# A decoder of six sublayers on one core: counting the next sequence's choices inside the FFN, and a new order of the pieces of two streams

## The reference

```python
x = _layernorm(x + mamba(x))                        # x: 16 sequences x 256 tokens x 256
x = _layernorm(x + latent_xattn(x, ctx, indices))   # indices: 16 x 256 x 64 choices of keys
x = _layernorm(x + ffn(x))                          # layernorm, int8-like quantisation, gelu
x = _layernorm(x + self_attention(x))
x = _layernorm(x + cross_attention(x, ctx))
x = _layernorm(x + moe(x))                          # 6 of 8 experts, and a shared one
```

## Time and profile before

| what | value |
|---|---|
| median of 3 runs | 4313.35 us (4283.68 to 4314.45) |
| the profiled execution, time | 4321.18 us |
| the profiled execution, span from first to last instruction | 4319.4 us |
| mean granted clock | 0.827 |
| TensorE / VectorE / ScalarE / GpSimd busy | 82% / 69% / 45% / 15% |

### The profile page before, as it was taken

The page is one execution under the profiler, slowest core; times in us unless marked ns, Lnnn a source line. Parts: engine busy times, 40 slices in busy tenths (PEclk is TensorE's granted clock), DMA queues, the critical chain, the costliest instruction groups (busy, mean ns, idle before and its releaser), DMA issues.

```text
span 4319.4 us, 57512 instructions
## 1 busy us (share of the span) xinstructions
PE 3553.2 (82%) x21234; PEld 2309.6 (53%) x21250; DVE 3000.4 (69%) x6506; ACT 1938.5 (45%) x4415; POOL 650.9 (15%) x516
## 2 busy tenths in 40 slices
PE   2668888888888888888888888878888888888977
PEld 1345645555565655645555564655645555564644
DVE  6586786848678585785858768586785858678532
ACT  2245454544545444453544535444453544545423
POOL 1112030301203021030200203011030201203000
PEclk7568989787897877888788888989888797897878
DMA  7233261514416152261523516153261524417101
GB/s 237 77 93 120 73 187 59 169 59 124 130 54 186 69 142 84 80 186 52 155 73 103 152 54 184 42 155 100 87 180 52 160 68 123 132 58 204 42 14 39
DMA packets 205689, 470.84 MB, mean 109 GB/s; under 512 B 23712, under 2 KB 43808, under 8 KB 190688
## 3 DMA queue, kind: packets, MB, share of 16 engines
q1 hardware_dynamic: 205408, 467.17, 35.7%
HBM read 446.11 MB, written 20.97 MB: 108 GB/s over the span
## 4 chain that ended last, share of the span: by engine, by line
PE 59%; DVE 26%; ACT 7%; issue 5%; DMA 3%; POOL 0%; SPq 0%; DVEq 0%; POOLq 0%; ACTq 0%
PE ps L593 7%; PE ps L574 5%; DVE region_x L1351 5%; PE ps L761 4%; PE ps L815 4%; PE ps L605 4%; PE ps L775 4%; PE ps L742 3%; PE ps L681 3%; PE ps L796 3%; DVE region_x L1338 3%; PE ps L464 3%; DMA region_x<-rows_of_dt 3%; PE ps L521 2%; DVE nm L1388 2%
## 5 line engine op out<-in xcount | busy, mean ns | idle before, releaser
L1148 POOL TENSOR_TENSOR region_x<-region_x 128x512 f32<-128x512 f32 x512 | 650.7, 1271 | 3327.8 <-DVE region_x L1351 3327.8
L1351 DVE TENSOR_TENSOR_SCAN region_x<-ps,region_x 128x512 f32<-128x512 f32 x512 | 622.6, 1216 | 67.0 <-ACT ps L965 67.0
L965 ACT ACTIVATE ps<-region_x,aneg 128x255 f32<-128x255 f32 x1024 | 443.2, 470 | 492.8 <-DVE region_x L1351 369.9
L1338 DVE TENSOR_TENSOR region_x<-region_x,ps 128x512 f32<-128x512 f32 x512 | 342.0, 668 | 42.8 <-PE ps L521 22.9
L1384 DVE CUSTOM_DVE_ANT_0 region_x<-ps,mask 128x256 f32<-128x256 f32 x512 | 185.9, 420 | 219.8 <-issue 219.4
L1075 ACT ACTIVATE region_y<-ps,rmax 128x256 f32<-128x256 f32 x512 | 235.2, 480 | 218.9 <-DVE rmax L1476 218.9
L815 PE MATMUL ps<-xTy,wide 128*128 128x256 f32 x1280 | 316.9, 397 | 3.5 <-DVE region_y L1535 3.5
L593 PE MATMUL ps<-region_y 32*128 32x256 f32 x1024 | 235.3, 601 | 86.5 <-ACT region_y L1001 52.3
L1401 DVE SCALAR_TENSOR_TENSOR region_x<-region_x,cntk 128x512 f32<-128x512 f32 x256 | 165.3, 687 | 196.5 <-ACT region_x L1001 196.5
L815 PEld LDWEIGHTS ps<-xTy,wide 128*128 128x128 f32 x1280 | 242.0, 196 | 52.9 <-issue 15.0
L1091 ACT ACTIVATE region_y<-ps 128x512 f32<-128x512 f32 x256 | 140.7, 595 | 284.7 <-PE ps L764 284.7
(11 more groups left out here) (244 smaller groups left out, 6632.2 us busy)
## 6 DMA issues: line engine op xcount, KB each, us to landing
region_x<-rows_of_dt SPq DMA_DIRECT2D x1024, 256.0 KB, 4.7
wide<-in_wgate SPq DMA_DIRECT2D x16, 1280.0 KB, 5.7
wide<-in_wup SPq DMA_DIRECT2D x16, 1280.0 KB, 8.4
down<-in_wmoe SPq DMA_DIRECT2D x16, 1280.0 KB, 5.5
wide<-in_wq SPq DMA_DIRECT2D x16, 1024.0 KB, 4.7
wide<-in_wk SPq DMA_DIRECT2D x16, 1024.0 KB, 7.4
wide<-in_wv SPq DMA_DIRECT2D x16, 1024.0 KB, 9.5
down<-in_wo SPq DMA_DIRECT2D x16, 1024.0 KB, 4.8
```

Source lines behind the costliest of these rows:

```text
L965: last = f(ps[:, 1 + 2 * (k % 2), m * T + 1:(m + 1) * T], dt_rep[k % SLOTS][:, m, 1:T], ACT.Exp, scale=aneg[:, k, m:m + 1])
L1148: nc.gpsimd.tensor_tensor(hbuf[k % HSLOTS], hbuf[k % HSLOTS], csb.unsqueeze(1).to_broadcast([P, 2, T]), ALU.mult).then_inc(hc_ready, 1)
L1338: tt_(hbuf[k % HSLOTS], dtx_rep[k % SLOTS], ps[:, 2, 0:T].unsqueeze(1).to_broadcast([P, 2, T]), ALU.mult).then_inc(dbx, 1)
L1351: nc.vector.tensor_tensor_scan(flat(hbuf[k % HSLOTS]), ps[:, 1 + 2 * (k % 2), :], flat(hbuf[k % HSLOTS]), 0.0, ALU.mult, ALU.add).then_inc ...
```

## The change

**Counting.** `digits` and `one_hots` of sequence i+1 now stand in `ffn` of sequence i on VectorE (digits and quarter 0 ahead of `f_h`, quarter 1 behind it, quarters 2 and 3 behind the quantisation), the 128 small matmuls in TensorE's `ffn` (quarters 0 and 1 behind w1, with a wait for both `f_h`; quarter 2 behind w2) and, quarter 3, behind the first projection of `mamba`. Their copies on ScalarE move alike. Turning the table, the mask and the last copy stay in `mamba`. Sequence 0 is counted before anything else.

**In-projection.** Its first two pieces no longer wait for `X.sum_read`; only the third does. The FFN's last sum and norm (`ffn_end`) run in two pieces inside the next `mamba` on VectorE, around the convolution.

**dt.** Low-rank part and rows of C are separate pieces, dt comes before B's columns, softplus's `sp_u` is made before Ln is there. SyncE stores the first half, reads back four units, and stores the second half then; the read waits for the first half only (units 0 to 15 use only that). In the scans the product of the next unit and the scan are separate pieces.

**Order.** Before, self-attention of y began with the low-rank part of the next-but-one `mamba`, and MoE ran beside the end of latent attention and the beginning of the FFN. Now y begins when that `mamba` has turned its counts. On TensorE: all of q, k, v and six score pieces come ahead of the first sum over states; cross-attention's output (L796) and the router come behind latent attention's output; the gate and up products stand beside the FFN's w1, counting and w2; the down product comes ahead of the last turning of the counts. On VectorE: self-attention's eight maxima stand between scans 1 and 6, its output pieces behind scans 19, 21 and 22, cross-attention's residual in the first norm of the FFN, MoE's products between the pieces of the FFN, MoE's residual in the middle of softplus, and `s.QT` (L1450) ahead of the first product. On SyncE the load of `wo2` stands between units 0 and 1 of the read-back, the store of the output at unit 8.

```diff
@@ first_half on SyncE @@
+                yield from store_half(0)
                 for k in range(UNITS):
...
+                    if k == SLOTS:
+                        yield from store_half(1)
+                    if k == 0 or k == UNITS // 2:
+                        sp.wait_ge(dt_stored[0], at(i, 32, 16 if k == 0 else 32))
@@ mamba on TensorE @@
+                pe.wait_ge(xT_loaded, at(i, 16, 16))
+                projected(0)
+                if i:
+                    yield from counted(i, 3, 4)
+                else:
+                    yield
+                yield
+                projected(1)
                 yield
                 if i:
                     pe.wait_ge(X.sum_read, at(i - 1, 3, 3))
+                projected(2)
...
+                pe.wait_ge(cnt_sb, at(i, 4, 4))
+                projected(3)
...
+                yield from counts_turned(i)
+                yield from counts_by_key(i)
@@ ffn on TensorE @@
+                if i + 1 < B:
+                    pe.wait_ge(f_h, at(i, TT, 2))
+                    yield from counted(i + 1, 0, 2)
...
                 last.then_inc(X.sum_ps, 1)
+                if i + 1 < B:
+                    yield from counted(i + 1, 2, 3)
@@ mamba on ScalarE @@
+                    if half == 0:
+                        yield
+                        if i:
+                            count_copy(i, 3)
+                        yield
+                        if i:
+                            rstd_guess_of(X, i - 1, before, 5)
+                            before.close()
+                        table(SILU_SET)
@@ mamba on VectorE @@
+            def mamba(i, c, before):
+                yield
+                next(before, None)
+                yield
                 c.link(nc.vector.memset(xin[:, :, 0:TAPS - 1], 0.0))
...
+                yield
+                next(before, None)
...
+                yield
+                masks(i)
                 for half in range(2):
                     ms = slice(2 * half, 2 * half + 2)
+                    if half:
+                        yield
+                        counts_by_key(i)
+                    yield
+                    v.wait_ge(dt_exp, at(i, 2, half + 1))
+                    c.link(ts(sp_u[:, ms], sp_e[:, ms], 1.0, None, ALU.add))
+                    c.did(stt(sp_u[:, ms], sp_u[:, ms], 1.0, sp_e[:, ms], ALU.subtract, ALU.subtract))
                     yield
                     v.wait_ge(dt_ln, at(i, 2, half + 1))
...
+                    if k == 2:
+                        for stored_rows in dt_stored:
+                            v.wait_ge(stored_rows, at(i, 32, 32))
@@ ffn on VectorE @@
+                yield
+                if i + 1 < B:
+                    digits(i + 1)
+                yield
+                if i + 1 < B:
+                    one_hots(0)
                 v.wait_ge(rows_loaded, at(i, 48, 48))
...
+                if i + 1 < B:
+                    one_hots(1)
...
+                for r in (2, 3):
+                    yield
+                    if i + 1 < B:
+                        one_hots(r)
                 yield
                 c.link(tt_(x, x, W["fb2"][:].unsqueeze(1).to_broadcast([P, TT, D]), ALU.add))
-                yield
+
+            def ffn_end(i):
...
@@ ORDER @@
-    "sp": (127, "x11 y1 x4 y5 x56"),
+    "sp": (136, "x6 y4 x5 y1 x16 y1 x44"),
-    "pe": (70, "x2 y2 x7 y2 x2 y2 x6 y4 x1 y8 x1 y2 x1 y5 x1 y5 x1 y4 x1 y6 x1 y6 x2 y2 x2 y2 x1 y1 x1 y1 x4 y1 x1 "
...
+    "pe": (77, "y11 x1 y7 x1 y2 x1 y5 x1 y4 x1 y7 x1 y5 x1 y2 x1 y1 x1 y1 x1 y2 x1 y1 x1 y2 x3 y1 x2 y1 x1 y1 x3 y3 "
...
+    "act": (92, "y1 x3 y1 x7 y2 x1 y2 x3 y3 x2 y1 x2 y4 x1 y1 x1 y4 x1 y2 x3 y3 x3 y1 x1 y1 x1 y2 x1 y3 x5 y1 x2 y2 "
...
+    "v": (138, "y1 x6 y1 x2 y1 x2 y2 x1 y2 x3 y3 x27 y1 x4 y1 x2 y1 x17 y3 x1 y1 x1 y1 x1 y1 x1 y3 x2 y1 x1 y1 x1 y1 "
...
```

More of the change, by code:

```diff
@@ L880, in all_first @@
             def all_first():
+                for _ in counted(0, 0, 4):
+                    pass
                 for i in range(B):
@@ L1124, in all_first @@
             def all_first():
+                for r in range(4):
+                    count_copy(0, r)
+                before = None
                 for i in range(B):
                     c = Chain(act, ax_step, i, A_STEPS)
-                    yield from mamba(i, c)
+                    yield from mamba(i, c, before)
                     yield from latent(i, c)
                     yield from ffn(i, c)
-                    c.close()
+                    before = c
+                yield
+                rstd_guess_of(X, B - 1, before, 5)
+                before.close()
             def all_second():
@@ L1545, in all_first @@
             def all_first():
+                digits(0)
+                for r in range(4):
+                    one_hots(r)
+                before = iter(())
                 for i in range(B):
                     c = Chain(v, vx_step, i, X_STEPS)
-                    yield from mamba(i, c)
+                    yield from mamba(i, c, before)
                     if i == 0:
@@ L1553, in all_first @@
                     c.close()
+                    before = ffn_end(i)
+                for _ in range(2):
+                    yield
+                    next(before, None)
             def all_second():
```

236 lines of the change are left out of this document (129 added, 107 removed), and 10 rows, old and new, of the table ORDER.

## The result

| | before | after |
|---|---|---|
| median of the runs | 4303.72 us | 4199.96 us (4191.22 to 4220.75) |
| profiled execution, span | 4319.4 us | 4189.4 us |
| start to the first end of an FFN | 247.7 us | 255.9 us |
| mean period | 258.0 us | 248.3 us |
| behind the last end of an FFN | 201.6 us | 209.7 us |

The ratio is 0.9767, 95% interval 0.9734 to 0.9800: faster by 2.3%. The forecast was no measurable change, 4330 us; the range of 4195 to 4455 us held the time at its very end.

The account below looks back on a forecast made before the run. VectorE sets four stages of a period, TensorE the middle. Terms -9 + 8.6 - 16 + 5 + 12.3 = +0.9 us, times 15 = +14, ends +3: 4330 us, no measurable change (0.34); 8-in-10 range 4195 to 4455 us.

Parts of the forecast that it names:

- the wait for the down product: Front: VectorE waits in the middle of softplus, before MoE's residual, from about 21.3 to 25.2 us.
- VectorE's idle time in the front and the FFN's first half: Sign for the forecast: some 18 us instead of 9.6 before; otherwise the forecast fails.
- Rival 3: Front: slower, down product over 1 us later than forecast delays VectorE directly; +8 us per period, 4435 us; chance 0.19.
- rival 4: Middle: slower, latent attention's chain sets it, so it shrinks by 8 only; +9 us per period, 4450 us; chance 0.12.
- the middle: Cross-attention beside latent attention, set by TensorE: 12.7 us of work leaves at 1.31 us per us; term -16 us.
- The bound of -20: Middle: the far bound on the -16 us term; the other bound was -8, where latent attention's chain decides.
- rivals 1 and 2: Faster: 1, TensorE's clock holds in scans, 4212 us, 0.22; 2, middle at its bound, front's wait absorbed, 4227 us, 0.13.
- Rival 1: Scans: TensorE keeps its clock, scans end 6 us earlier, middle 2; -7 us per period, 4212 us; chance 0.22.
- The front: End of the FFN to the first scan: first scan at 36 us instead of 45; term -9 us.
- The stores of dt cost nothing: Front: the half-wise store's gain is hidden by the rest of the front; first half lands by 27, needed at 34.
- The FFN's first half: VectorE waits for latent attention's output (4.9 us), ScalarE (1.6), router (1.5); TensorE isn't late; term +5 us.
- Sum +3: Ends of the run, outside the periods: counting first +3, one front without MoE -6, last self-attention +6 us.

Follow-up runs that it names:

- mix_as_before: Kernel after, with the middle's pieces of cross-attention and latent attention mixed as in the kernel before; what left the middle stays out: 4513.8 us, ratio 1.0496.
- warm_middle: Kernel before plus 21 unread fp32 products, three ahead of each of latent attention's last seven score pieces for the maximum: 4304.2 us, ratio 1.0013.
- dt_whole_wo2_late: Kernel after, with all dt stores ahead of the first read-back and the 1 MB wo2 load moved to unit 10: 4290.5 us, ratio 0.9965.
- dt_whole: Kernel after, with all four dt stores ahead of the first read-back, which waits for them all: 4348.9 us, ratio 1.0086.
- down_later: Kernel after, with MoE's residual and norm behind softplus's second half and the counts' last turning between the down product's halves: 4201.4 us, ratio 0.9745.
- new_middle_2: Kernel before with the new order of middle and FFN, counting matmuls ahead of down product and self-attention, 1 MB load at unit 10: 4389.9 us, ratio 1.0200.
- digits_mid: Kernel after, 1 MB load at unit 10, digits in the middle, only the fourth one-hot quarter left in the FFN's second half: 4153.8 us, ratio 0.9662.
- ffn_first: digits_mid with the FFN's quantisation, turning and w1 ahead of cross-attention's residual, router turning and MoE's first gate product: 4116.4 us, ratio 0.9556.
- wo2_late: Kernel after, with the 1 MB load of cross-attention's output weights at unit 10 and the output store at unit 11: 4186.3 us, ratio 0.9734.
- sum_read_back: Kernel after, with the first in-projection piece again waiting for the FFN's last sum to be read, MoE's last weighting product ahead: 4271.1 us, ratio 0.9922.
- warm_scans: Kernel after plus 52 unread fp32 products ahead of self-attention's score pieces for the maximum and the exponentials: 4446.2 us, ratio 1.0321.

## Why the prediction was wrong

**What held.** The stages and their order, the period as the unit, the wait for the down product (4.30 us, as forecast), the first scan 36 us behind L1437, over 80 us of scans (83.5), no hole on TensorE in the FFN's second half (idle for 3.8 us, 8.0 before). VectorE's idle time in the front and the FFN's first half, on which I had set the forecast, was 22.2 us where I had 18, and its work 3.1 us less than I had. Rival 3's point was not reached, rival 4's premise, that latent attention's chain sets the middle, fits mix_as_before, but the new order shortened that chain.

**The step that failed** is the middle: "The stage runs 92.6 us for 70.5 us of work at full clock ..., 1.31 us per us, which makes -16.6. I take -16". The stage's length was spread over TensorE's pieces as a rate, and the work that leaves was priced at it; so idle time and low clock were taken to shrink in proportion to the work. The work itself came out nearly as I had it, 11.8 us less at full clock (72.6 to 60.8) where I had 12.7. The rate allowed 3.9 us beyond that; the clock gave 9.3 (12.5 to 3.3) and the idle time 4.5 (9.6 to 5.1). I had held the mix for fixed and let the new order change only what stands in the stage. mix_as_before shows what a fixed mix gives: 3.7 us, and no clock at all; the new mix cut the wait of latent attention behind cross-attention (9.2 us of idle time against mix_as_before) and the low clock (9.6). So the rate is wrong both ways, too high with the old mix and too low with the new. The bound of -20 has no working of its own and was no bound. I also took one period for the stage: 92.6 where the mean is 94.7.

**The range** was too narrow by its own rule: five terms with bounds of 5 us each, erring independently, make 11 us a period and not 9, so 168 us and not 135. That the time lies 5 us inside it is luck. The times of rivals 1 and 2 are 2 us too high by their own terms (-8 x 15 is -120, not -118; -7 x 15 is -105, not -103).

**Rival 1** was the right mechanism in the wrong stage. TensorE's clock did not stay up in the scans (43.6 us low, more than the 29.6 before) but in the middle. The Trainium skill (TensorE: Matmul & The Clock Gate, "HAM oscillation — how this bites in real kernels") puts the low clock down to idle gaps of TensorE and advises to arrange the loop so that it stays warm. The middle agrees (idle time 9.6 to 5.1 us, 21 us less at 1.2 GHz), and so do both halves of the FFN (the first: idle 1.9 to 7.1, low 0.0 to 10.9; the second: idle 8.0 to 3.8, low 9.4 to 2.0). The scans don't agree: scans 9 to 20 are at the low clock for 23 of 31 us with TensorE busy for 26.8. In warm_middle, feeding it alone cost as much as it gave. The low clock's price in this stage, 0.45 us for each us of it, is the number that I lacked. It stood in the trace of before, in middles of the same instructions that take 88 and 101 us at granted clocks of 0.93 and 0.79:

```profile
620.00:708.00 88.00, 78.80 (x555) 50.88 (x552) 42.58 (x140) 43.61 (x123) 1.27 (x1) 0.93 0.16 62
...
1648.00:1749.00 101.00, 91.80 (x550) 56.29 (x547) 42.07 (x138) 43.71 (x123) 0.89 (x1) 0.79 0.13 51
```

**Right for another reason.** The front: "The stores of dt cost nothing", their gain "hidden by the rest of the front". dt_whole_wo2_late shows that the halves carry 5.0 of its 10.1 us, and dt_whole that the front would lose 9.2 without them and with the load where it is. I had put the down product's wait on VectorE's account with a price for each us; down_later shows a price of none, as the row behind it is TensorE's. The FFN's first half: I named VectorE's waits; the half is 28.5 to 28.7 us with 14.5, 18.0 or 19.8 us of VectorE's work in it (new_middle_2, the kernel after, digits_mid), and ffn_first shows that TensorE's order sets it. That both terms fitted is luck: the sizes were right, the engine was not.

**Taken apart in steps.** The new order alone costs 4.9 us a period (258.0 to 262.9: middle -24.4, scans +10.5, front +8.0, FFN +10.8); counting and in-projection out of the front, with what else the change does there, give back 8.3 (dt_whole_wo2_late, 254.6), the halves of dt 6.2 (wo2_late, 248.5). Neither side gains alone: the new order on the old code is 2.0% slower than before, the new code with the old middle 5.4%. sum_read_back puts 5.9 us on the in-projection; that leaves little for the counting's own place, though such steps need not add. The ends were off by 13 us: "Sum +3" was +16 (8.2 ahead, 8.1 behind); no run took this apart.

## What to carry to other kernels

Split a stage into busy time at full clock, idle time and time at the low clock before pricing a change of order, and ask of each whether the new order keeps it; a rate over the whole stage assumes that it does. The same stage in all periods of one trace gives the price of the clock without another run. Before a wait is priced, look for the row that stands behind it on the engine that ends it: the waits for the down product, for q and for the sums over states vanished or moved here, and no run gained by it.

## What the runs showed of the hardware

In the middle one microsecond at 1.2 GHz cost 0.41 us (the line through the 14 middles of mix_as_before), 0.45 (the kernel before) and 0.34 to 0.47 (warm_middle); in the scans, where VectorE is busy for 73 of 84 us, at most 0.33 (warm_scans). Middles of the same instructions took 84 or 102 us at granted clocks of 0.94 and 0.73. In scans 9 to 20 of the kernel after TensorE was busy for 26.8 of 31 us and yet at the low clock for 23; 11.7 us of the busy time were products of 32 rows and 13.6 products of 32 columns. 21 full-height products (9.8 us) raised a middle's clock from 0.85 to 0.97. That the low clock there comes of the small products is not shown, nor what makes it fall for 10 us in one middle of mix_as_before and for 55 in another. A 1 MB load ahead of a read of 256 KB in one queue: that read's user waited 7.9 us, and 2.6 in the same period with the load elsewhere.
